# Cross-attention scores: two block-diagonal products of 64 rows into two banks, in place of one of 128 rows into one

## The reference

```python
x = x + xcond0(layernorm(x), ctx)      # cross attention, 77 keys a batch
x = x + ffn0(layernorm(x))             # 64 channels, each its own little relu network
x = x + xcond1(layernorm(x), ctx)      # cross attention again, other weights
x = x + ffn1(x)                        # window attention, and routed attention on chosen rows

def xcond(q, ctx, tau, delta):         # 16 heads of 32
    qh, kh, vh = heads(q @ Wq.T + bq), heads(ctx @ Wk.T + bk), heads(ctx @ Wv.T + bv)
    scores = einsum("blhe,bshe->bhls", qh, kh) * tau + delta
    a = softmax(scores / sqrt(32))
    return einsum("bhls,bshd->blhd", a, vh) @ Wo.T + bo
```

## Time and profile before

| what | us |
|---|---|
| median of 3 runs | 4210.44 |
| lowest and highest of them | 4210.44 and 4210.71 |
| the profiled execution | 4207.2 |
| its span in the profile | 4205.1 |

### The profile page before, as it was taken

How to read it: one execution, slowest core, us unless ns; L and a number is a source line. 1 busy time by engine, 2 the same in 40 slices (tenths; PEclk the granted TensorE clock), 3 DMA queues, 4 the chain that set the end, 5 groups by cost and what they waited for, 6 DMA issues and landing times.

```text
span 4205.1 us, 51100 instructions
## 1 busy us (share of the span) xinstructions
PE 3705.1 (88%) x19906; PEld 2919.3 (69%) x19906; DVE 2283.2 (54%) x4629; ACT 1642.5 (39%) x2603; POOL 1085.5 (26%) x852
## 2 busy tenths in 40 slices
PE   6989888989878999999988999998899999978888
PEld 3867677767666777877766676766677677756666
DVE  3565656565665766667653445445455654453333
ACT  1444444444444444444423555552132222232222
POOL 1333333323222333333320222221122222250110
PEclk8989898989888999999988999999899999987879
DMA  3010100101111110111021111110022111030000
GB/s 119 24 42 22 34 29 24 39 21 41 35 43 41 42 38 30 38 41 40 31 74 34 46 43 46 53 48 33 32 78 68 58 63 43 33 121 11 21 26 11
DMA packets 106279, 180.02 MB, mean 43 GB/s; under 512 B 29598, under 2 KB 30366, under 8 KB 104504
## 3 DMA queue, kind: packets, MB, share of 16 engines
q1 hardware_dynamic: 101496, 162.07, 11.6%
q0 software_dynamic: 3968, 10.50, 0.8%
q10 hardware_dynamic: 576, 4.19, 0.3%
HBM read 106.09 MB, written 70.64 MB: 42 GB/s over the span
## 4 chain that ended last, share of the span: by engine, by line
PE 66%; DVE 14%; issue 10%; ACT 5%; POOL 3%; DMA 2%; SPq 0%; POOLq 0%; ACTq 0%; DVEq 0%
PE ps L307 11%; PE ps L309 10%; PE ps L308 10%; PE ps L302 7%; PE ps L314 7%; PE ps L522 5%; PE ps L1224 4%; PE ps L1208 3%; PE ps L511 3%; DVE st L587 2%; PE ps L1189 2%; PE ps L1754 2%; PE ps L1768 1%; DVE sTa L710 1%; DVE Sb L666 1%
## 5 line engine op out<-in xcount | busy, mean ns | idle before, releaser
L902 POOL TENSOR_TENSOR Sb<-Sb,mx 128x1232 f32<-128x1232 f32 x128 | 288.9, 2257 | 987.9 <-DVE mx L671 987.9
L522 PEld LDWEIGHTS ps<-VB,PT 103*128 103x128 f32 x3072 | 400.4, 206 | 73.7 <-ACT PT L835 57.0
L1592 POOL TENSOR_TENSOR Sw<-Sw,mw 128x2048 f32<-128x2048 f32 x64 | 233.7, 3651 | 833.0 <-DVE mw L1314 833.0
L522 PE MATMUL ps<-VB,PT 103*128 103x66 f32 x3072 | 399.3, 287 | 50.0 <-ACT PT L835 50.0
L302 PE MATMUL ps<-KB,QT 128*128 128x308 f32 x1024 | 353.1, 450 | 1.6 <-ACT QT L796 1.6
L314 PE MATMUL ps<-ident,xn 128*128 128x128 f32 x1120 | 193.4, 304 | 155.8 <-DVE xn L1271 73.3
L314 PEld LDWEIGHTS ps<-ident,xn 128*128 128x128 f32 x1120 | 151.2, 159 | 213.9 <-issue 86.4
L796 ACT ACTIVATE QT<-ps,bq 128x512 f32<-128x512 f32 x128 | 88.0, 688 | 518.9 <-PE ps L309 518.9
L835 ACT COPY PT<-ps 103x384 f32<-103x384 f32 x512 | 239.9, 480 | 95.5 <-PE ps L511 94.9
L511 PEld LDWEIGHTS ps<-ident,Sb 128*103 128x103 f32 x1536 | 214.3, 173 | 83.1 <-DVE Sb L666 35.9
L666 DVE TENSOR_TENSOR Sb<-ps,dlt 128x308 f32<-128x308 f32 x512 | 225.9, 470 | 84.5 <-PE ps L302 83.4
(11 more groups left out here) (271 smaller groups left out, 8256.0 us busy)
## 6 DMA issues: line engine op xcount, KB each, us to landing
XB<-in_x SPq DMA_DIRECT2D x16, 1024.0 KB, 5.4
x_scratch<-XB SPq DMA_DIRECT2D x16, 1024.0 KB, 4.3
XB<-x_scratch SPq DMA_DIRECT2D x16, 1024.0 KB, 5.9
x_scratch<-XB SPq DMA_DIRECT2D x64, 256.0 KB, 2.0
XL<-x_scratch SPq DMA_DIRECT2D x64, 256.0 KB, 2.8
XY<-x_scratch SPq DMA_DIRECT2D x64, 256.0 KB, 2.8
y_scratch<-XY SPq DMA_DIRECT2D x64, 256.0 KB, 2.0
out<-yo SPq DMA_DIRECT2D x64, 256.0 KB, 2.0
```

The lines of the kernel that those rows point to most:

```text
L522: m = PE.matmul(ps[:, p, o:o + 66], PT[:, 3 * g + c, :], VB[kvi(n) % 2][:, g, c, :], start=(j == 0 and c == 0), stop=(j == 1 and c == 2), ...
L902: G.tensor_tensor(sv, sv, last(mx[:, n % 2, :], NK), ALU.subtract).then_inc(g_sub, 1)
```

## The change

A group's product is split in two: rows 0 to 63 with the first two heads, rows 64 to 127 with the other two. In each half the keys stand block-diagonally over two heads, so each product has 154 columns. The two results go to two neighbouring banks, at columns 0 to 153 of each, and VectorE's addition reads both banks in one instruction of as many elements as before. KB has half as many columns; its four copies are as large as they were. The semaphore pe_s is raised by the second product of the pair, so it counts as before.

With it goes a new division of the banks: scores take turns over the pairs (0, 1) and (2, 3), all other results of the stage over the four banks 4 to 7.

```diff
--- before.py
+++ after.py
@@ -358,7 +358,7 @@
         cF = sb("cF", [128, D])
         rt_ = sb("rt", [128, 2, D])
         KT = [sb(f"KT{L}", [128, 4, B * NK]) for L in (0, 1)]
-        KB = [sb(f"KB{s}", [128, 4, 4 * NK]) for s in (0, 1)]
+        KB = [sb(f"KB{s}", [128, 4, 2 * NK]) for s in (0, 1)]
         VB = [sb(f"VB{s}", [103, 4, 3, 66]) for s in (0, 1)]
         Wout = sb("Wout", [128, D])
         fcol = sb("fcol", [128, 32])
@@ -407,7 +407,7 @@
 
         WQ, WO, WIN = (4, 16), (8, 20), 12
 
-        banks = Banks(range(8))
+        banks, pairs_a = Banks((4, 5, 6, 7)), Banks((0, 2))
         freed = {"K": lambda L, c: (v_kv, 8 * L + c + 1),
                  "V": lambda L, b: (v_kv, 8 * L + b + 5),
                  "b2": lambda: (v_feed, 3),
@@ -424,13 +424,13 @@
                  "wbo": lambda: (v_bl, 3)}
 
         def take(kind, *key):
-            bank, before = banks.take((kind, *key))
+            bank, before = (pairs_a if kind == "S" else banks).take((kind, *key))
             if before:
                 pe.wait_ge(*freed[before[0]](*before[1:]))
             return bank
 
         def bank(kind, *key):
-            return banks.at[kind, *key]
+            return (pairs_a if kind == "S" else banks).at[kind, *key]
 
         def ring(u):
 
@@ -500,8 +500,11 @@
                 p = take("S", n, g)
                 pe.wait_ge(a_q, 4 * u + 4)
                 pe.wait_ge(v_kb, 4 * (kvi(n) + 1))
-                mms(ps[:, p, 0:308], [(QT[:, u % 2, g, 128 * t:128 * t + 128],
-                                       KB[kvi(n) % 2][:, g, :])]).then_inc(pe_s, 1)
+                for h in range(2):
+                    r = slice(64 * h, 64 * h + 64)
+                    m = PE.matmul(ps[:, p + h, 0:2 * NK], QT[r, u % 2, g, 128 * t:128 * t + 128],
+                                  KB[kvi(n) % 2][r, g, :], start=True, stop=True)
+                m.then_inc(pe_s, 1)
 
             def ptrans(n, g):
                 p = take("PT", n, g)
@@ -644,7 +647,7 @@
                 ve.wait_ge(v_kv, 8 * L + 4)
                 ve.wait_ge(pe_s, 64 * (i - 1))
                 for k in range(4):
-                    V.tensor_copy(KB[i % 2][32 * k:32 * k + 32, :, NK * k:NK * k + NK],
+                    V.tensor_copy(KB[i % 2][32 * k:32 * k + 32, :, NK * (k % 2):NK * (k % 2) + NK],
                                   KT[L][32 * k:32 * k + 32, :, NK * b:NK * b + NK]).then_inc(v_kb, 1)
 
             def new_q(k):
@@ -663,8 +666,9 @@
                 ve.wait_ge(pe_pt, 4 * (n - 1))
                 ve.wait_ge(v_init, 3)
                 s = n % 2
+                p = bank("S", n, g)
                 V.tensor_tensor(Sb[:, s, 308 * g:308 * g + 308].rearrange("p (i k) -> p i k", i=4),
-                                ps[:, bank("S", n, g), 0:308].rearrange("p (i k) -> p i k", i=4),
+                                ps[:, p:p + 2, 0:2 * NK].rearrange("p b (i k) -> p b i k", i=2),
                                 mid(dlt[:, batch(n), :], 4), ALU.add).then_inc(v_sadd, 1)
                 if g == 3:
                     ve.wait_ge(v_sadd, 4 * n + 4)
```

## The result

| | before | with the change |
|---|---|---|
| median of 4 runs each, us | 4210.57 | 4369.98 |
| lowest and highest | 4210.44 and 4212.30 | 4369.14 and 4372.66 |
| profiled execution's span | 4205.1 | 4367.0 |
| mean granted clock over the span | 0.925 | 0.909 |

The change makes the kernel slower by 159.4 us: a ratio of 1.0384, with a 95% interval of 1.0367 to 1.0400.

What follows compares the result with a forecast made beforehand. The prediction took TensorE, busy 88% of 4205.1 us, to bound the kernel. Terms 88 + 15 + 2 - 6 = +99 on the profiled 4207.2, plus 3.2 to the median, gave 4309 us, range 4250 to 4380.

Steps and rivals of the forecast that it cites:

- Two signs: First stage: tiles 0 to 63 were to grow by 10 to 30 us, tiles 64 to 127 by 60 to 110.
- Bank stalls of the second part: Tiles 64 to 127: scores g = 2 wait for VectorE's late delta add of g = 0; +88 us (+30 to +106).
- The step that shortened 6.6 us in four tiles to 5.5: Tiles 64 to 127: tile 84's net 1.06 us comes off tile 85's stall, as a stall shortens the next.
- The clock: TensorE's granted clock, tiles 64 to 127: more short waits could lower it; priced at 0, bounds 0 and +34 us.
- Bank stalls of the first part: Tiles 0 to 63: same wait for the delta add, VectorE mostly in time; +15 us, bounds +5 and +24.
- Four banks for the rest: Non-score results: P's transpose waits for OTp's low part, hidden behind the other wait; +2 us, bounds 0 and +10.
- The product: Score products on TensorE: halves run at once, but switching costs 0.35 us a run; -6 us, bounds -17 and +4.
- Rival 1: Score products: 64-row switches cost nothing and stalls are mostly swallowed, so faster, 4112 us; chance 4%.
- Rival 3: Score products: the two halves don't run at once, +134 us instead of -6, giving 4449 us; chance 2%.
- Rival 2: TensorE's bank waits: new stalls only replace others, both bank terms vanish, 4204 to 4214 us; chance 5%.
- Rival 4: First stage: bank stalls at their upper bounds and the clock down to 0.91, 4388 us; 4% beyond 4380.

Runs made afterwards that it cites:

- e1: Kernel before with its 128-row product; scores take turns over banks 0 and 2, all else over 4 to 7: 4359.8 us, ratio 1.0348.
- e5: e1 plus two useless products in TensorE's wait ahead of scores g = 2, from tile 64 on: 4319.8 us, ratio 1.0269.
- e2: e1 with all results other than scores taking turns over six banks instead of four: 4341.5 us, ratio 1.0305.
- e12: Changed kernel with the routing sums moved from the head of the turn to behind scores g = 1: 4244.1 us, ratio 1.0087.
- e8: Kernel before, each score product cut into two of 154 columns over all 128 rows, same bank: 4203.6 us, ratio 0.9992.
- e10: Kernel before with useless 512-column products filling TensorE's two long waits in tiles 0 to 63: 4167.6 us, ratio 0.9912.

## Why the prediction was right, and where its sizes were off

- **Direction and place: right; the size was near the edge.** Forecast 4309 (4250 to 4380), measured 4370. The wait for "DVE Sb" was to be 100 to 140 us, mostly past 1250: it is 119.7 there and 20.7 ahead of it, 140.4 in all. Waits for OTp were to stay under 20: 1.8 and 0.4. The score records run in pairs. Later stages grew by 6 us. Two signs failed: the first part was to grow by 10 to 30 us and grew by 42, the second by 60 to 110 and grew by 113.
- **Bank stalls of the second part, +88: the mechanism right, the size near.** 119.7 less the 34 that TensorE waited before is 86, but other waits became shorter: TensorE's idle time rose by 75 in the change and by 70 in e1. e5, with the clock back at 0.96, leaves 69 us over before. e1 and e2 have the whole +113 without the new product, and e12 has none of it with it. The step that shortened 6.6 us in four tiles to 5.5 (tile 85's lateness partly its own) could not be tested by itself. Nor do the rows give its 1.06 us for tile 84: 1.42 less a quarter of the 2.1 is 0.9, which makes the term some 3 us larger.
- **The clock, 0 (bounds 0 and +34): mis-sized.** This is the term that failed most. The prediction named the effect ("more short waits could bring the lower level more often") and put it at 0 without a reason. I had said that under 0.92 in the second part it would be wrong; it is 0.90. e5 puts it at about 45 us, above my upper bound, and so does TensorE's busy time in e1, 44 us longer for the same work. I had reckoned with "some 4% longer" as the worst, from 0.91 in the first part. By the clock records TensorE stood at the lower level for 85 us of the second part before and for 222 now. Waits of 2 us in nearly every turn brought that: with e5's products in them it is 85 again.
- **Bank stalls of the first part, +15: right in sum.** e2 over before: 14.5. It is made of 21 us more idle time and 7 less busy time, since TensorE stood at the lower level for 205 us of the first part there and for 236 before; so close a match is in part luck.
- **Four banks for the rest, +2 (0 to +10): mis-sized.** e1 over e2: 18 us, all in the first part. I had looked only at what P's transposes wait for in a plain turn (OTp, which was right). In turns where the preparation of a block is mixed in, they wait for xT, by their weight loads, 11 to 13 us. The other 5 to 7 I did not find as a wait. TensorE stood at the lower level for 14 us longer there in e1 than in e2 (218.5 us against 204.8), which could be as much; that is argued, not shown.
- **The product, -6 (-17 to +4): mis-sized.** The change over e1: +10 to +15. Per row the forecast was close: 0.64 and 0.88 against 0.61 and 0.87, so +0.07 a tile instead of +0.01 to +0.02. At the lower clock a run of two groups took 1.52 and one of a single group 1.07 at most, within the ranges given. By these costs the term would be some 9 us if all were at the full clock, and about none with the share at the lower one; measured are 10, all of them in the first part. The rest may be the clock again: over the span 0.909 against e1's 0.916 means some 60 us more at the lower level. That is argued, not shown. In e8 the split alone costs nothing, so the switches are what the product pays with. That was the mechanism forecast; what came out otherwise is its sum. The rule that changing the tiling mode drains TensorE (the Trainium skill, TensorEngine Tiling (Array Packing), Key Properties) agrees: 0.20 in and 0.15 to 0.18 out, three times a tile.
- **Rival 1 (the packing pays): wrong** by the same 0.35 us. **Rival 3 (the halves don't run at once): wrong,** a run of one group would have taken 0.87. **Rival 2 (stalls only take the place of others): wrong** for this order, since VectorE's 94 us of spare time lay ahead of the delta add, not behind it. e12 shows what it would have taken to make it right in the second part. **Rival 4** had the right two parts with the sizes the other way round: the stall not at its upper bound, the clock beyond its own.

By measured parts the whole is: 69 stall and about 45 clock in the second part, 14.5 + 18 + 10 in the first, and 6 in stages B and C, whose cause I did not look for. Together 162, the difference of the two spans. Against the forecast's terms that is 45 more for the clock, 16 more for the ring of four, 16 more for the product and 6 for the later stages, and 19 less for the stall of the second part. That the time still fell inside the range, 10 us from its upper end, owes something to this last one: too large a stall covered a part of the missing clock.

What stays open: whether four banks for the scores with the old product, and four for the rest, would do; that was not tried. Nor was e12's order in the kernel before, or e12's order with e10's filling.

## What to carry to other kernels

A ring of result banks is only as deep as its reader is prompt: before giving a kind of result fewer banks, look at what stands ahead of its reader in program order, above all at a wait (here VectorE for zx) that has nothing to do with the bank; moving that one item gave back 117 us in the second part here. A new wait on TensorE can have two prices, its own length and the clock behind it, and here the second was two thirds of the first. A product of 64 rows between products of 128 pays only if the run is long: at 0.35 us for entering and leaving, and at the full clock, a run of one float32 group of 308 columns lost 0.12 us and a run of two won 0.16.

## What the runs showed of the hardware

- Useless products in TensorE's waits made two kernels faster by 40 us and one by 31, the granted clock of the part going from 0.90 or 0.91 to 0.96 or 0.97.
- Waits of 2 us on average, the longest of 3.3, 58 of them in 64 turns, took the granted clock from 0.96 to 0.91 (e1, second part), and the same products then kept TensorE busy for 44 us more in 1065.
- A VectorE sum with two SBUF inputs, started 0.56 us into GpSimd's subtraction, took 2.62 us instead of 0.68, and GpSimd 2.63 instead of 2.26.
- Entering and leaving 64-row products costs 0.20 and 0.15 to 0.18 us at the full clock; two halves in different banks then stream at once.
- 512 products of 308 columns at full height, cut into 1024 of 154, took no more time (e8: 0.9992 of the kernel before).
